# Second attention with the normalisation on ScalarE and three of four value copies on VectorE, and stores of the left-over tokens spread out in the last MLP

## What is computed

```python
h = tokens(x)                                   # 64 x 197 x 192
h = h + attn_0(layernorm(h))                    # single head
h = h + ffn_0(layernorm(h))                     # 192 -> 768 -> 192
# second attention: 12 heads of 64
qkv = layernorm(h) @ W_qkv                      # 192 -> 3 * 768
s = einsum('ghid,ghjd->ghij', q, k) * 64**-0.5  # within one image
h = h + (softmax(s) @ v) @ W_0
# last MLP: activations and weights rounded to whole numbers of -8..7
xq = round(clip(layernorm(h) / a1, -8, 7))
x1 = clip(gelu(xq @ wq1.T * alpha_w1 * a1 + b1), -10, 10)
out = h + round(clip(x1 / a2, -8, 7)) @ wq2.T * alpha_w2 * a2 + b2
```

## Time and profile before

| | us |
|---|---|
| median of three runs | 2365.83 (2365.36 to 2367.9) |
| profiled execution, its own time | 2370.66 |
| its span, first to last instruction | 2368.9 |
| second attention, within the span | about 764 to 2160 |
| last MLP, within the span | about 2160 to 2369 |

### The profile page before, as it was taken

How to read it: one execution, slowest core, us unless ns; L and a number is a source line. 1 busy time by engine, 2 the same in 40 slices (tenths; PEclk the granted TensorE clock), 3 DMA queues, 4 the chain that set the end, 5 groups by cost and what they waited for, 6 DMA issues and landing times. The chain is left out here.

```text
span 2368.9 us, 76500 instructions
## 1 busy us (share of the span) xinstructions
PE 2161.4 (91%) x25422; PEld 1694.2 (72%) x25422; DVE 1996.3 (84%) x4966; ACT 2009.4 (85%) x5695; POOL 1712.6 (72%) x2215
## 2 busy tenths in 40 slices
PE   6899999999999799999999999999999999988876
PEld 5788876888777577777777777777777777765554
DVE  5777777889786789998999989999899998986997
ACT  4688876777774799999999999999999999995986
POOL 5778852333333589899998989989899898993554
PEclk9999999999999999999999999999999999998999
DMA  6344411000000376666666666666666666672111
GB/s 191 109 123 126 130 34 29 6 5 35 15 13 6 60 124 122 121 119 123 120 123 121 119 123 120 123 121 119 123 119 125 120 120 123 118 128 43 56 46 61
DMA packets 734156, 222.65 MB, mean 94 GB/s; under 512 B 667590, under 2 KB 732720, under 8 KB 733808
## 3 DMA queue, kind: packets, MB, share of 16 engines
q1 hardware_dynamic: 733776, 221.36, 45.9%
q10 hardware_dynamic: 288, 0.20, 0.0%
HBM read 46.49 MB, written 9.68 MB: 24 GB/s over the span
## 5 line engine op out<-in xcount | busy, mean ns | idle before, releaser
L1524 POOL TENSOR_TENSOR b_pr<-b_pr,fc 128x394 f32<-128x394 f32 (+1 forms) x768 | 652.0, 870 | 124.0 <-DVE fc L1444 124.0
L1373 ACT ACTIVATE b_pr<-b_scores,fc 128x197 f32<-128x197 f32 (+1 forms) x1536 | 632.1, 440 | 2.6 <-issue 1.2
L1509 POOL TENSOR_TENSOR b_halves<-b_pr,b_halves 128x394 f16<-128x394 f32 (+1 forms) x640 | 564.9, 908 | 31.9 <-ACT b_halves L1342 27.7
L1281 PE MATMUL b_banks<-fp,wqkv 128*128 128x197 f16 x3840 | 377.7, 249 | 42.8 <-DVE b_qk L1428 38.8
L1438 DVE TENSOR_REDUCE fc<-b_scores 128x2 f32<-128x394 f32 x768 | 395.7, 556 | 3.5 <-PE b_scores L1299 1.4
L1281 PEld LDWEIGHTS b_banks<-fp,wqkv 128*128 128x128 f16 x3840 | 320.0, 98 | 83.9 <-DVE b_qk L1428 60.6
L1342 ACT ACTIVATE b_halves<-b_pr 128x788 f16<-128x788 f32 x384 | 342.8, 893 | 4.5 <-POOL b_pr L1524 3.5
L1373 ACT ACTIVATION_READ_ACCUMULATOR b_pr<-b_scores,fc 128x1 f32 (+1 forms) x1536 | 341.0, 222 | 0.0
L985 POOL TENSOR_TENSOR h<-h,fp_bias 69x192 f32 (+3 forms) x128 | 133.4, 1069 | 266.9 <-DVE m_xn L139 266.9
L1428 DVE SCALAR_TENSOR_TENSOR b_qk<-b_banks,b_qk 128x394 f16<-128x394 f32 x384 | 214.9, 560 | 101.7 <-ACT b_qk L1356 101.5
L1288 PE MATMUL b_banks<-wqkv,fp 128*128 128x384 f16 (+1 forms) x1280 | 254.6, 330 | 40.7 <-DVE h L1463 38.8
(11 more groups left out here) (252 smaller groups left out, 4378.5 us busy)
## 6 DMA issues: line engine op xcount, KB each, us to landing
patches<-in_x SPq DMA_DIRECT2D x64, 588.0 KB, 4.3
b_pt<-b_halves SPq DMA_TRANSPOSE x384, 3.1
out<-z_res SPq DMA_DIRECT2D x62, 96.0 KB
fc<-b_halves SPq DMA_TRANSPOSE x192, 3.2
fp<-b_halves SPq DMA_TRANSPOSE x192, 3.2
m_raw_weights<-in_wqkv SPq DMA_DIRECT2D x2, 1152.0 KB, 6.9
out<-z_res SPq DMA_DIRECT2D x32, 51.8 KB
h<-h SPq DMA_DIRECT2D x32, 44.2 KB
```

What stands on the lines that cost most here:

```text
L1281: last = t.matmul(out[:, g * SEQ:(g + 1) * SEQ], w[:, (2 * n + g) * P:(2 * n + g + 1) * P], x, start=(j == 0), stop=(j == 4))
L1373: last = nc.scalar.activation(pr[n % 3][0:ROWS[c], c, e, :], scores[n % 2][0:ROWS[c], e, c * SEQ:(c + 1) * SEQ], ACT.Exp, bias=nmx[n % 2][ ...
L1509: nc.gpsimd.tensor_tensor(halves[n % 3][0:ROWS[c], c, 1, :, 0:SEQ], pr[n % 3][0:ROWS[c], c], halves[n % 3][0:ROWS[c], c, 0, :, 0:SEQ], ALU ...
L1524: last = nc.gpsimd.tensor_tensor(p, p, inv, ALU.mult)
```

## The change

In the second attention:

- `n` moves from VectorE to ScalarE: four activations with the function Identity, scale `rstd` and bias `shift`, two pointers per instruction. `shift` is -mean times rstd, made once for all images by one VectorE instruction ahead of the loop. ScalarE waits for `filled` before the first, and in later ones for `x_ready` as VectorE did.
- the high parts of `v1`, `v2` and `v3` move from ScalarE to VectorE, as step `u` (a tensor_copy out of PSUM), with the waits that ScalarE had. `v0` stays. The counters of the high parts are two, one for each engine.
- all four orders are new.

In the last MLP the left-over group has a third `z_res` buffer and a semaphore of its own; its 32 stores are issued four at a time behind those of groups 13 to 20.

```diff
-    PE_ORDER = ("v0 m4^^ s4^ v1 q4 m5^^ s5^ v2 w^^ q5 s0 v3 x' m0^ m1^ s1 q0' q1' "
-                "m2^ s2 q2' q3' s3 m3^").split()
-    ACT_ORDER = ("o1^ v0' e3 v1' h1 q4' o2^ h2 v2' e4 e5 q5' h3 v3' x'' h4 o0 e0' h5 "
-                 "q0'' q1'' e1' h0' q2'' e2' q3''").split()
-    DVE_ORDER = ("m5^ v2 n' r4^ w^^ r5^ q5 m0 v3 x' l4^ r0 m1 q0' o0^ q1' m2 r1 q2' "
-                 "m3 q3' o1^ v0' r2 m4 r3 v1' q4' o2^").split()
-    POOL_ORDER = ("p3^ p4^ l3^ p5^ k^^ p0 l5^ l0 p1 p2 l1 l2").split()
+    PE_ORDER = ("m3^^ q3 v1 s4^ m4^^ q4 m5^^ v2 s5^ q5 v3 s0 w^^ x' m0^ s1 m1^ q0' "
+                "q1' s2 m2^ v0' q2' s3").split()
+    ACT_ORDER = ("q4' o2^ h2 e4 q5' h3 e5 h4 x'' e0' o0 h5 q0'' q1'' e1' h0' v0'' "
+                 "q2'' e2' h1' q3'' o1 n''' e3'").split()
+    DVE_ORDER = ("q5 u3 v3 m0 r5^ w^^ x' l4^ r0 m1 q0' q1' r1 o0^ m2 v0' q2' m3 r2 "
+                 "q3' u1' o1^ v1' m4 r3 q4' u2' o2^ v2' m5 r4").split()
+    POOL_ORDER = ("p0^ l5^^ p1^ l0^ p2^ l1^ p3^ k^^ l2^ p4^ l3^ p5^").split()
...
+                    if kind == "n":
+                        if later(img):
+                            act.wait_ge(x_ready, img)
+                        elif img == 0:
+                            act.wait_ge(filled, 1)
+                        for c in range(2):
+                            rows, j = slice(0, ROWS[c]), bass.ds(2 * img + c, 1)
+                            move, scale = S["shift"][rows, j], S["rstd"][rows, j]
+                            twice = h[rows, img, c, P:D].unsqueeze(1).to_broadcast([ROWS[c], 2, LO])
+                            nc.scalar.activation(xn[rows, c, 0:P], h[rows, img, c, 0:P], ACT.Identity, bias=move, scale=scale)
+                            last = nc.scalar.activation(xn[rows, c, P:2 * P].rearrange("p (a b) -> p a b", a=2), twice, ACT.Identity, bias=move, scale=scale)
+                        last.then_inc(xn_made, 1)
...
-                last.then_inc(filled, 1)
+                    v.memset(rsum[r][:], 1.0)
+                v.scalar_tensor_tensor(out=S["shift"][:], in0=S["mean"][:], scalar=-1.0, in1=S["rstd"][:], op0=ALU.mult, op1=ALU.mult).then_inc(filled, 1)
...
+                    if kind == "u":
+                        dve.wait_ge(v_ready, 4 * img + n + 1)
+                        if n % 2 == 0 and later(PAIRS * (img - 2) + 3):
+                            dve.wait_ge(mixed, PAIRS * (img - 2) + 3 * (n // 2) + 3)
+                        c, col, at = n % 2, (n // 2) * VH, job_bank("v", n)
+                        v.tensor_copy(val[odd][0:ROWS[c], 0, c, col:col + VH], banks[0:ROWS[c], at, 0:VH]).then_inc(high_by_v, 1)
...
-        return 16 * sum(len(pieces(tile)) for g in range(last % 2, last + 1, 2) for tile in groups[g])
+        return 16 * sum(len(pieces(tile)) for g in range(last % 2, last + 1, 2) if g != LEFT for tile in groups[g])
...
-        res = [sb(f"z_res{b}", [P, GROUP, D]) for b in range(2)]
+        res = [sb(f"z_res{b}", [P, GROUP, D]) for b in range(3)]
...
-                    b = g % 2
+                    b = 2 if g == LEFT else g % 2
                     dve.wait_ge(made_y, g + 1)
-                    if g >= 2:
+                    if g >= 2 and g != LEFT:
                         dve.wait_ge(stored[b], stores(g - 2))
...
+                    if g > LEFT:
+                        for k, (i, lo, hi, row) in left[LEFT_STORES * (g - LEFT - 1):LEFT_STORES * (g - LEFT)]:
+                            sp.dma_start(out[i, lo:hi, :], res[2][row:row + hi - lo, k, :]).then_inc(left_stored, 16)
```

More of the change, by code:

```diff
@@ L1169, in attention_1 @@
         freed = [sem(f"b_freed{c}") for c in range(2)]
-        (xn_made, xt_hi, xt_split, qk_hi, qk_split, v_hi, v_split, inverted, prob_made,
+        (xn_made, xt_hi, xt_split, qk_hi, qk_split, v_split, inverted, prob_made,
          high_made, mixed, ot_hi, ot_split, filled, cleared, x_ready, q_ready, v_ready, w_ready, h_updated) = map(sem, (
-             "b_xn_made", "b_xt_hi", "b_xt_split", "b_qk_hi", "b_qk_split", "b_v_hi", "b_v_split",
+             "b_xn_made", "b_xt_hi", "b_xt_split", "b_qk_hi", "b_qk_split", "b_v_split",
              "b_inverted", "b_prob_made", "b_high_made", "b_mixed", "b_ot_hi",
              "b_ot_split", "b_filled", "b_cleared", "b_x_ready", "b_q_ready", "b_v_ready", "b_w_ready", "b_h_updated"))
+        high_by_s, high_by_v = sem("b_high_by_s"), sem("b_high_by_v")
+        V_ON_VECTOR = sorted(number(s) for s in DVE_ORDER if s[0] == "u")
+        V_ON_SCALAR = [n for n in range(4) if n not in V_ON_VECTOR]
         LOW_ON_POOL = sorted(number(s) for s in POOL_ORDER if s[0] == "l")
@@ L1197, in low_made, with v_high @@
             return signal, 2 * len(by) * (img + before) + 2 * by.index(n) + c + 1
+        def v_high(img, n):
+            signal, by = (high_by_v, V_ON_VECTOR) if n in V_ON_VECTOR else (high_by_s, V_ON_SCALAR)
+            return signal, len(by) * img + by.index(n) + 1
         def turned(img, n):
@@ L1361, in step @@
                         c, col = n % 2, (n // 2) * VH
-                        copy(val[odd][0:ROWS[c], 0, c, col:col + VH], banks[0:ROWS[c], k, 0:VH]).then_inc(v_hi, 1)
+                        copy(val[odd][0:ROWS[c], 0, c, col:col + VH], banks[0:ROWS[c], k, 0:VH]).then_inc(high_by_s, 1)
                     elif kind == "e":
@@ L1430, in step @@
                     elif kind == "v":
-                        dve.wait_ge(v_hi, 4 * img + n + 1)
+                        dve.wait_ge(*v_high(img, n))
                         c, col = n % 2, (n // 2) * VH
@@ L1538, in mlp_1 @@
     assert all(len(g) == GROUP for g in groups) and len(rows_left) < GROUP
-    groups.insert(len(groups) // 2, [("left", k) for k in range(len(rows_left))])
+    LEFT = len(groups) // 2
+    groups.insert(LEFT, [("left", k) for k in range(len(rows_left))])
     count = len(groups)
+    LEFT_STORES = 4
+    assert LEFT_STORES * (count - 1 - LEFT) >= n_img // 2
     def rows(tile):
@@ L1688, in _ @@
             def _(sp):
+                left = [(k, piece) for k, tile in enumerate(groups[LEFT]) for piece in pieces(tile)]
                 def store(g):
-                    b = g % 2
                     sp.wait_ge(h_done, g + 1)
@@ L1693, in store @@
                         for i, lo, hi, row in pieces(tile):
-                            if g == count - 1 and k % 2:
+                            if g == LEFT or (g == count - 1 and k % 2):
                                 continue
-                            sp.dma_start(out[i, lo:hi, :], res[b][row:row + hi - lo, k, :]).then_inc(stored[b], 16)
+                            sp.dma_start(out[i, lo:hi, :], res[g % 2][row:row + hi - lo, k, :]).then_inc(stored[g % 2], 16)
+                    if g > LEFT:
+                        for k, (i, lo, hi, row) in left[LEFT_STORES * (g - LEFT - 1):LEFT_STORES * (g - LEFT)]:
+                            sp.dma_start(out[i, lo:hi, :], res[2][row:row + hi - lo, k, :]).then_inc(left_stored, 16)
                 in_turn([(store, 0)])
+                sp.wait_ge(left_stored, 16 * len(left))
                 for g in (count - 2, count - 1):
```

4 lines of the change are left out of this document (2 added, 2 removed).

## The result

The changed kernel takes 2353.26 us (median, 2350.23 to 2354.77), the kernel before 2366.86 in the same comparison: a ratio of 0.9936, 95% interval 0.9923 to 0.9948, or 13.6 us less where 31 were forecast. Faster was right, and the size was less than half. The profiled execution took 2353.93 (span 2352.1, mean granted clock 0.991).

What follows compares the result with a forecast made beforehand. A chain through all four nearly full engines was taken to set each round. 26.2 us from the attention's rounds plus 5.8 from the last MLP minus 1.0 once, 31.0 off 2365.83, gave 2335, range 2312 to 2368.

Steps and rivals of the forecast that it cites:

- the walk: Second attention, a round followed step by step in the new orders: odd 21.4, even 19.9, 20.7 us per image against 21.13.
- e0: An exponential step on ScalarE, right behind x in the walked round; one of six e per image, 1.60 us for four.
- e5: An exponential step on ScalarE, between h3 and h4; it needs GpSimd's l2, with 0.05 us added for this and l4.
- as feared: GpSimd in odd rounds: k is ahead of l2, which e5 needs, and waits for o2; 0.05 us added with l4.
- the prediction's end: Signs of being wrong: n over 0.49 us a start, or waits at e for GpSimd's low halves.
- Rival 2: Second attention: most waits stay, 1.1 to 1.4 us per image, by thin margins or n at 0.45; 2349 to 2367, chance 0.16.
- Rival 1: Second attention: ScalarE's 1.74 us of waits stay and 0.43 us of work per image is added; 2387, chance 0.12.
- rival 3: Second attention: odd and even rounds even out to a mean of 20.3 us, 55.4 us less, 2310; chance 0.08.
- the path of w: Second attention before the change: n's 2.66 us on VectorE delay w, and TensorE waits 1.26 us before v3.
- the exchange: Second attention: n to ScalarE, three value copies to VectorE; ScalarE 0.43 us more, VectorE 1.26 us less per image.
- the ring: A round as a chain through all engines; in the experiments a closed one, whose last step releases the next round's first.
- The stall: Last MLP: VectorE's 3.56 us wait before finish of group 14 for the left-over group's 32 stores; 5.8 us gain forecast.

Runs made afterwards that it cites:

- dve_turned: The changed kernel with the same order of work on VectorE, but the loop's end put before r1 instead of before q5: 2349.21 us, ratio 0.9919.
- swap_old: The changed kernel with the four orders of the kernel before, n at the end of ScalarE's round, u1 to u3 ahead of their v on VectorE: 2401.03 us.
- n_back: The changed kernel with its new orders, but n taken back to VectorE, between q1 and r1: 2343.67 us, ratio 0.9903 to the kernel before.
- w_short: The changed kernel with the third product of w left out in the loop's odd images, 24 matmuls and not 36: 2321.18 us, ratio 0.9811.
- n_half: The changed kernel with the second chunk's two Identity activations of n left out in the loop's 60 images: 2306.93 us, ratio 0.9748.
- n_split_turned: As n_split, with VectorE's round cut ahead of r1 and not ahead of q5: 2316.78 us, ratio 0.9786 to the kernel before.
- n_split: The changed kernel with the second chunk's two instructions of n on VectorE, between q1 and r1, the first chunk's on ScalarE: 2321.95 us, ratio 0.9812.

## Why the forecast gain was too high

**The step that failed** is the walk's waits: 20.70 us per round forecast, 21.03 measured, 61 x 0.33 = 20 us. ScalarE's work in it was right. Odd rounds take 21.95 us (e2 at 1300.66, then at 1322.61) with 1.61 + 0.38 + 0.09 of waits, so 19.87 of work, even ones 20.12 with 0.27 of waits, so 19.85; the forecast was 19.83. The added work came as forecast, and the waits didn't fall as forecast: 1.74 us per image before, 0.87 forecast, 1.17 measured. Waits over two rounds were forecast at 1.43 + 0.13 + 0.10 + 0.10 = 1.76 and are 2.35. The 0.59:

- x, 1.61 and not 1.43. From q5 to w's start on TensorE it takes 1.52 us (1310.02 to 1311.54), not 1.16: 0.20 is the loop's end on VectorE, which dve_turned took away, 0.08 a copy whose record is 0.58 and not 0.50, and 0.07 more lie between VectorE's end and w's start (0.13, not 0.06). w and x came 0.07 sooner than walked and ScalarE needed 0.11 longer.
- q1, 0.38 and not 0.13. The low part of x waits on VectorE behind w's sum and statistics, 1.33 us from 1314.85 to 1316.18, while x's high part is there at 1315.72. On TensorE q0 starts 0.85 behind m1's start (1316.21 to 1317.06), and in the even round 0.64 (1336.44 to 1337.08), so this holds it up by 0.21. I had placed w and x on VectorE and not timed them. No run took this wait away alone.
- small waits at e0 and e5, 0.36 and not 0.20. The e5 of odd rounds waits 0.09 for l2, behind `k`, as feared. The e0 of even rounds waits 0.27 for GpSimd's l3, which the walk left out; of such waits the prediction's end said that they would prove it wrong. GpSimd's l3 ends at 1336.09, and e0 starts at 1336.12:

```profile
1334.30 1.79 POOL L1529 TENSOR_TENSOR b_halves<-b_pr,b_halves 128x394 f16<-128x394 f32 x2
```

```profile
1336.12 0.43 ACT L1393 ACTIVATE b_pr<-b_scores,fc 128x197 f32<-128x197 f32 x1
```

**Why so small an error cost so much.** The forecast gain was 0.43 us per image. An error of 0.3 in a walk of 20.7 us is 1.5%, and it took three quarters of the gain there. Rival 2 had 1.1 to 1.4 us of waits per image, 2349 to 2367; measured are 1.17 us and 2353.26. The size of that rival is what happened, but hardly its cause: n was at its forecast price, and low halves on GpSimd gave 0.16 of the 0.59. The other 0.43 lie at x and q1, which the walk had priced and not doubted. Rival 1 did not come, since the waits did shrink, and rival 3 did not either: odd and even rounds are 1.83 us apart, where the walk had 1.5.

**Costs, point by point.** n 0.385 a start: right. u3 to v3 0.57 (1311.33 to 1311.90) where 0.46 + 0.12 was taken: right. VectorE's loss, 2.5 over two images: 3.25; the low half of pair 4 helps, which in odd rounds now falls where GpSimd is idle and takes 1.04 us (1316.94), in even ones 1.76 (1336.83). The gain from taking n out of the path of w: right in kind, for TensorE's wait before v3 fell from 1.26 to 0.37, but only with the new places; swap_old takes n out of that path too and loses 34 us. I had argued that moved work is small beside the orders, and then let the exchange carry the story. The start of the attention: 2.1 us longer to the first maximum, 1.0 forecast. The end, from the last maximum: 3.0 shorter, none forecast, with TensorE's clock as one visible difference (below). Between first and last maximum 9.7 us were won, of which 61 x 0.105 = 6.4 are the steady rounds; the 3.3 in the first and last images were not tested. So the steady rounds missed by 20 us and the attention by only 14.6 (10.6 for 25.2): what wasn't forecast at its two ends and in the tail made up for the rest, which is luck.

**Rival 1's rule.** n_back bears on the rule of the Trainium skill, VectorE: DVE Perf Modes, Specifications, that VectorE is closer to SBUF and ScalarE to PSUM. For n (SBUF to SBUF) the sign agrees, 10 us for VectorE; for the value copies (out of PSUM) the runs are against it, 50 us for VectorE. My reading is that what counts is which engine has the ring at that moment; the rule by itself doesn't give the sign.

**Last MLP.** The stall is gone, seven steps of 7.24 us, 5.5 us in the trace against 5.8; the mechanism and the size hold there, within what the runs can tell. The 5.8 had a misreading in it: the row at 2334.65 is the second half of group 20, whose first half starts 0.47 earlier. From first half to first half the seven steps took 56.03 us, 5.3 more than 50.7, and that is what came back in them (50.69).

```profile
2334.18 1.01 DVE L1654 TENSOR_TENSOR z_res<-z_bank_y,q_scale 128x384 f32<-128x384 f32 x2
```

**What stays open.** The new orders with neither part of the exchange, and the old ones with the value copies alone, were not run, so the share of the orders by themselves isn't known, nor why the exchange loses in the old ones. A fourth buffer for the probabilities, which would take GpSimd's waits away, does not fit in SBUF and wasn't tried.

## What to carry to other kernels

Walk the whole ring with every engine on it timed, the one that gives the low part too, before a small difference is multiplied by the number of rounds; then ask of each moved block what stands behind it in its new queue and who needs that. A visible wait in a ring isn't spare time: w_short and n_half shortened its two sides, and both counted in full. A price read on one instruction belongs to the moment in which it ran, so look at what the other engines do in the new place.

## What the runs showed of the hardware

- The end of a loop on VectorE is seen as about 0.2 us before the first instruction of the next pass where VectorE has run dry (q5 in after, 0.24 us behind its copy and not 0.04), and it is in the path where that one is (dve_turned, 4 us; n_split_turned, 5 us). Behind an instruction that still runs it isn't seen: 0.84 us to r1 in n_split_turned and in n_split.
- On ScalarE the duration in a record grows along an unbroken stretch while the distance of the starts doesn't: an exponential is 0.51 at 1309.62, 15.6 us behind the last wait (e0 of the even round, whose record at 1294.06 is 0.43), and 0.42 at 1312.46, both 0.40 before the next start. So the distance is what an instruction takes of its own engine. The record's end is what another engine sees: in dve_turned VectorE's q5 starts 0.03 us behind the end of the copy's 0.58.
- TensorE's granted clock fell in the attention's tail, for a shorter time in after. In windows of 5 us it is 0.50 in three of before (2130 to 2145) and 0.51 and 0.50 in two of after (2120 to 2130). The last window at 1.00 ahead of the fall has TensorE busy for 2.90 of 5 us in before (2120 to 2125) and 2.40 of 5 in after (2115 to 2120). Two windows of 10 us, first before, then after (PE, PEld, DVE, ACT, POOL, clock):

```profile
2135.00:2145.00 10.00, 7.03 (x57) 5.54 (x58) 4.97 (x10) 6.06 (x20) 10.00 (x12) 0.50 0.82 119
```

```profile
2125.00:2135.00 10.00, 7.52 (x84) 6.28 (x83) 5.01 (x11) 7.47 (x23) 9.53 (x11) 0.73 0.68 125
```

In before, this stretch ran wholly at the lower of the two levels (0.50, 1.2 GHz), 57 matmuls in 7.03 us of busy time; after, part of it was at 2.4 GHz, 84 in 7.52. The two are not the same stretch of work. Whether the tail's 3 us are this alone wasn't tested.
